# A fused vision tower on one core: two moves in TensorE's order of the last stage

## The reference

```python
h = window_attention(x)                     # 8x8 windows, 8 heads, rotary positions
h = h + local_attention(layernorm(h))       # 1024 tokens, 7x7 neighbourhood mask
h = h + routed_ffn(layernorm(h))            # expert by block of tokens, 2 expert layers
h = h + retention(layernorm(h))             # (q k^T * 0.99^(i-j)) v, no softmax
h = h + binary_experts(layernorm(h))        # below

gate = sigmoid(x @ proj_w.T + proj_b) > 0.5          # 8 gates for each token
w = einsum('be,eio->bio', gate, weight)              # a 64x64 matrix for each token
y = einsum('bi,bio->bo', sign(x), sign(w)) * scale
```

## Time and profile before

| | |
|---|---|
| time of the runs | 1646.99 us median of 3 (1640.81 to 1647.67) |
| profiled execution | 1643.16 us, span 1641.4 us |
| TensorE busy | 1514.8 us (92%) |
| ScalarE busy | 1005.4 us (61%), 8 or 9 tenths in the final stage |
| VectorE busy | 1207.1 us (74%) |
| final stage, first unit to the end | 903.7 to 1641.4 us |

### The profile page before, as it was taken

How to read it: one execution, slowest core, us unless ns; L and a number is a source line. 1 busy time by engine, 2 the same in 40 slices (tenths; PEclk the granted TensorE clock), 3 DMA queues, 4 the chain that set the end, 5 groups by cost and what they waited for, 6 DMA issues and landing times.

```text
span 1641.4 us, 85558 instructions
## 1 busy us (share of the span) xinstructions
PE 1514.8 (92%) x30828; PEld 1091.4 (66%) x30828; DVE 1207.1 (74%) x3605; ACT 1005.4 (61%) x1925; POOL 616.0 (38%) x926
## 2 busy tenths in 40 slices
PE   6899999799999999999878999999999999999997
PEld 5677777577877887778767565656656565656652
DVE  2566666578888888888648787888788787888862
ACT  2444444345555554555412888888888888888886
POOL 4252233366666676666522222222222222222210
PEclk9899999899999999999989999999999999999995
DMA  4322222244444444444411545455555555455553
GB/s 142 68 51 48 48 47 42 59 125 128 130 127 127 126 125 127 130 126 129 119 31 36 91 78 91 82 86 86 82 90 78 93 79 91 81 87 85 83 88 52
DMA packets 146869, 147.46 MB, mean 90 GB/s; under 512 B 54898, under 2 KB 102258, under 8 KB 146546
## 3 DMA queue, kind: packets, MB, share of 16 engines
q1 hardware_dynamic: 137922, 117.38, 37.5%
q10 hardware_dynamic: 8880, 29.16, 6.1%
HBM read 66.48 MB, written 16.99 MB: 51 GB/s over the span
## 4 chain that ended last, share of the span: by engine, by line
PE 77%; ACT 9%; issue 6%; SPq 3%; DMA 2%; DVE 1%; POOL 1%; ACTq 0%; POOLq 0%; DVEq 0%
PE ps_D L954 10%; PE ps_D L859 8%; PE ps_OT L878 4%; ACT prob L1267 4%; PE ps_AV L973 4%; PE ps_AV L886 3%; PE ps_D L708 3%; PE ps_D L855 3%; ACT prob L1162 3%; PE ps_J L1033 2%; PE ps_J L1017 2%; PE ps_OT L1043 2%; PE ps_OT L788 2%; PE ps_J L1067 2%; PE ps_OT L1110 2%
## 5 line engine op out<-in xcount | busy, mean ns | idle before, releaser
L1267 ACT ACTIVATE prob<-ps_D 128x1024 bf16<-128x1024 f32 x448 | 459.1, 1028 | 114.8 <-PE ps_D L954 114.2
L1237 ACT ACTIVATE prob<-ps_D 100x512 f32<-100x512 f32 x256 | 139.0, 595 | 101.5 <-PE ps_D L859 101.5
L577 POOL TENSOR_TENSOR tile_a<-q_st,q_mask 128x512 f32<-128x512 f32 x128 | 135.3, 1057 | 144.6 <-PE ps_D L859 138.6
L859 PE MATMUL ps_D<-tile_a,key_patch 64*100 64x128 f32 x2048 | 172.3, 287 | 0.1
L1443 DVE TENSOR_REDUCE m_sb<-ps_D 128x4 f32<-128x400 f32 x256 | 134.4, 565 | 22.2 <-PE ps_D L836 22.2
L1390 DVE TENSOR_REDUCE top<-ps_D 128x8 f32<-128x512 f32 x128 | 79.4, 683 | 96.5 <-PE ps_D L686 96.5
L551 POOL TENSOR_TENSOR rstd_bin<-veps_bin,minus_half 128x2 f32<-128x2 f32 x64 | 44.2, 690 | 260.5 <-DVE veps_bin L1328 260.5
L551 POOL TENSOR_TENSOR rstd_ret<-veps_ret,minus_half 128x2 f32<-128x2 f32 x64 | 47.4, 740 | 243.7 <-DVE veps_ret L1328 243.7
L859 PEld LDWEIGHTS ps_D<-tile_a,key_patch 64*100 64x100 f32 x2048 | 132.2, 165 | 0.0
L855 PE MATMUL ps_D<-mT,key_rows 64*100 64x128 bf16 x1024 | 118.6, 227 | 4.5 <-ACT prob L1237 4.5
L954 PE MATMUL ps_D<-tile_b,w_parts 64*64 64x256 bf16 x2048 | 104.6, 288 | 15.7 <-ACT prob L1267 12.2
(11 more groups left out here) (188 smaller groups left out, 3855.6 us busy)
## 6 DMA issues: line engine op xcount, KB each, us to landing
tile_a<-xg SPq DMA_DIRECT2D x192, 128.0 KB, 4.3
tile_b<-xg SPq DMA_DIRECT2D x192, 128.0 KB, 4.5
key_st<-k_d SPq DMA_DIRECT2D x128, 162.0 KB, 3.1
tile_b<-v_d ACTq DMA_DIRECT2D x128, 120.0 KB
tile_b<-v_d ACTq DMA_DIRECT2D x64, 160.0 KB
w_exp<-experts SPq DMA_DIRECT2D x64, 129.0 KB, 2.3
xT<-in_x SPq DMA_DIRECT2D x32, 256.0 KB
tile_a<-rot SPq DMA_DIRECT2D x256, 16.0 KB
```

Source lines behind the costliest of these rows:

```text
L577: gp.tensor_tensor(q_block[:, par, :].rearrange("c (p h q) -> c p h q", h=NH, q=NQ)[:, own, :, :], q_st[:, par, :].rearrange("c (p a q) -> ...
L859: mm = pe.matmul(s_loc[x][0:NKL, u * P:(u + 1) * P], key_patch[rows_of(x), par, at * NKL:(at + 1) * NKL], q_block[rows_of(x), par, at * P: ...
L1237: act.activation(prob1[0:NKL, 2 * g + x, :], s_loc[x][0:NKL, :], ACT.Exp).then_inc(T2["exp_done"], 1)
L1267: act.activation(sgn[:, k % 4, :], unit(k, par)[:, :], ACT.Sign).then_inc(BN["sign"], 1)
```

## The change

On TensorE, two groups of instructions are written at another place of the step. Unit 4 with its wait now stands ahead of the first expert product and its waits; it stood behind it. The next strip's unit 0, with its waits for the landed transfer and for the sign of unit 6, now stands directly behind unit 7, ahead of the retention output; it stood behind it. Nothing is added or removed, and the queues of the other engines are the same. `weights(4, ...)` is the fifth unit, `weights(0, ...)` the first one.

```diff
@@ -1026,15 +1026,15 @@
+                if q is not None:
+                    signed(q, 2)
+                    weights(4, par, unit(4, par))
                 if f is not None:
                     pe.wait_ge(FF["w_in"], times((f + 1) * 16))
                     pe.wait_ge(FF["hid_sb"], times(f * 3 + 1))
                     settle(pe)
                     pe.matmul(bank["J1"][:, 0:256], w_exp[:, 0, 0:HID], hidT[:, 0, :], start=True, stop=True).then_inc(FF["hid_ps"], 1)
 
-                if q is not None:
-                    signed(q, 2)
-                    weights(4, par, unit(4, par))
@@ -1101,6 +1101,15 @@
                 if q is not None:
                     weights(7, par, unit(7, par))
+                if n is not None:
+                    if isinstance(n, int) and n == 0:
+                        pe.wait_ge(s_placed, 13)
+                        pe.wait_ge(s_clear, 4)
+                    pe.wait_ge(BN["x_in%d" % (1 - par)], times((n + 1 + par) * 48))
+                if q is not None:
+                    signed(q, 6)
+                if n is not None:
+                    weights(0, 1 - par, ring(8, par))
                 filling(j, 3)
                 if r is not None:
                     pe.wait_ge(RT["sd"], times(r + 1))
@@ -1110,15 +1119,6 @@
                     mm.then_inc(RT["out_ps"], 1)
-                if n is not None:
-                    ...
-                    weights(0, 1 - par, ring(8, par))
```

More of the change, by code:

```diff
@@ L1112, in strips @@
                     mm.then_inc(RT["out_ps"], 1)
-                if n is not None:
-                    if isinstance(n, int) and n == 0:
-                        pe.wait_ge(s_placed, 13)
-                        pe.wait_ge(s_clear, 4)
-                    pe.wait_ge(BN["x_in%d" % (1 - par)], times((n + 1 + par) * 48))
-                if q is not None:
-                    signed(q, 6)
-                if n is not None:
-                    weights(0, 1 - par, ring(8, par))
             staggered(pe, strips)
```

## The result

Before and after ran on one chip, four executions each: before 1647.33 us (1640.81 to 1656.44), after **1623.9 us** (1619.42 to 1630.01), both medians. The ratio is 0.9863, with a 95% interval of 0.9825 to 0.9901, so the change saves 16 to 29 us. Medians are of all executions of a kernel; the ratios leave out one slow execution of experiment 1 (1636.92 us, at a granted clock of 0.967). The prediction was 1637, with a range of 1630 to 1648. The direction held; the time lies outside the range, at its fast side, and the gain of the medians, 23.4 us, is two and a half times the 9.4 us of the sum.

A forecast was written before the change was run, and what follows sets the result against it. The prediction took a step's time as TensorE's own work (92% busy) plus its waits; -0.41 + 0.25 = -0.16 us a step, times 59, is -9.4 us, giving 1637.6, stated as 1637, 8-in-10 range 1630 to 1648.

The forecast's parts named there:

- the 9.4 us of the sum: Whole change: 0.41 won and 0.25 lost make -0.16 us a step, times 59 steps.
- part 2: Unit 4 ahead of the first expert product fills TensorE's wait for `hidT`; query-key product 0.41 us a step earlier.
- part 1: Unit 0 ahead of the retention output: unit 1 and the clip come later, 0.25 us a step lost (bounds 0.19, 0.31).
- The base of 0.19: At unit 0: TensorE stands 0.19 us for sign 6, formerly covered by the retention output, so unit 1 comes later.
- The addition of 0.06: At unit 0: started out of a wait, it may last 0.53 us for 0.41, adding 0.12 in every second step.
- The signs that were announced: Changed kernel's timeline: expected waits and distances around `hidT`, the query-key product, unit 0, sign 0 and clip; clip starts 11.38 us apart.
- Nothing gained: Rival: unit 1's delay of 0.31 and a gain of only 0.32 a step cancel; 1646 us, chance 0.25.
- Both idle times pay: Rival: 0.34 at unit 2 and 0.25 at the product both won each step; 1612 us, within a 0.10 chance.
- A new wait that costs more than the fill: Rival: unit 0 waits for sign 6, bringing unit 1 over 0.41 us late; 1655 us, chance of slower 0.10.
- the bound of 0.22 a step: Fast bound of the whole change's summed gain: -0.22 us a step, -13 us.
- the case beyond it: Whole kernel: more gained than summed, up to both idle times, chance 0.10.

The follow-up runs named there:

- experiment 1: Kernel before with only unit 4 moved ahead of the first expert product, unit 0 left behind the retention output: 1625.82 us, ratio 0.9883.
- experiment 9: Kernel before with only unit 4 moved, and four transfers of gated tokens a step for six (part of the result left out): 1615.4 us, ratio 0.9821.
- experiment 6: Changed kernel with two extra 64x64x256 matmuls between the first expert product and the query-key product: 1643.84 us, one execution.
- experiment 2: Kernel before with only unit 0 moved ahead of the retention output, unit 4 left behind the first expert product: 1653.82 us, ratio 1.0056.
- experiment 5: Changed kernel with two extra 64x64x256 matmuls inside unit 5: 1624.82 us, one execution.
- experiment 4: Kernel before with unit 4 early, the retention output's second half behind the next unit 1, and `reduce(q, 2)` behind unit 7: 1611.9 us, ratio 0.9811.
- experiment 10: Kernel of experiment 4 with gated-token transfers issued ahead of the result's store on SyncE, and `yo` made behind the state update: 1607.41 us, ratio 0.9764.

## Why the prediction was wrong, point by point

**The step that failed: part 2's term of 0.41.** I followed the chain to the start of the query-key product and stopped there, taking all behind it to move as a block. Up to that point it was right: unit 4 came 0.37 behind the transposes (forecast 0.37), the product 0.34 behind it (0.34), the query-key product 0.53 behind that (0.51); 0.39 won for 0.41. Behind that point another 0.10 was won, since the query-key product no longer follows a 64x64 unit. Measured alone the part is worth 0.50 (experiment 9), and experiment 6 gives the missing piece back when a unit's kind of product is put in again (0.11 behind the query-key product). The rows to see it were there: two products of the same shape, 0.67 and 0.70 long, each behind a wait or a unit. I used their overlap for the first and did not ask what the second would be with a new neighbour. Net of the 0.02 short of 0.41, this is 0.08 of the missing 0.14 a step.

**The term that was too large: part 1's 0.25.** The base of 0.19 was right within 0.01 (1.83 - 1.64). The addition of 0.06 was for a first unit that lasts 0.53 when it is started out of a wait. It did not come: unit 0 lasts 0.41, and so does unit 3, which now starts out of a wait of 0.48. This is the other 0.06. It was no price before the change either: unit 3 starts 0.47 behind unit 2 both in the step where unit 2 lasts 0.53 (1205.64 to 1206.11) and in the one where it lasts 0.41 (1217.24 to 1217.71), since the clip holds it. What makes a unit 0.53 long in some steps was not tried and stays open; it is not the wait alone.

**In sum**: forecast -0.41 + 0.25 = -0.16; shown -0.39 - 0.10 + 0.19 = -0.30. Times 59 this is -17.7 us, which with 0.14 a step more than forecast puts the time at 1637.6 - 8.3 = 1629. The measured median of 1623.9 is 5 below that, and the interval of the ratio (1618 to 1631 on the median of before) holds it. I don't explain the 5 us: it is within the scatter of the executions; between the two that were profiled, 4.3 us lay ahead of the first sign.

**The signs that were announced.** The wait for `hidT` is gone. The query-key product starts 0.80 behind the modelled end of the transposes (1205.94 + 0.44 to 1207.18; forecast 0.75 to 0.85). Unit 0 stands 0.19 for a sign, though as a distance and not as a printed wait. Sign 0 follows sign 7 without a gap, unit 3 still starts 0.14 behind the clip, and TensorE now waits for the clip. All came, and the length of the step alone was off, 11.24 for 11.38. Each sign stood at a place that I had costed already; none stood behind the last of them.

**The rivals.** Nothing gained: its terms were a loss of 0.31 and a gain of 0.32, and both lay off. Both idle times pay: its time, 1612, lies 12 us from the measured 1623.9 and my 1637 lies 13 from it, but its mechanism is refuted, since the idle time at unit 2 was worth nothing (experiment 2). A new wait that costs more than the fill: it needed unit 0 to wait 0.41, and it waits 0.19. The loss from that wait is real (experiment 2, slower by 0.56%), and part 2 more than makes up for it. One effect stood in none of my cases: in the length of a step the changed kernel is only 0.06 longer than unit 4's move alone (11.24 against 11.18), and the two times can't be told apart (0.9863 and 0.9883, intervals overlap), since unit 4's gain alone runs into the landing of the transfers in every second step. Beside part 2, part 1 thus costs 0.06 and not its own 0.2.

**The range.** Its fast end came from the bound of 0.22 a step, and the case beyond it had 0.10. The bounds covered the terms that I had, and nothing covered a term that was missing. That a change moves a product of another shape out of a row of its like could be seen in the order of TensorE, and was worth a bound.

## What to carry to other kernels

When an instruction group is moved on TensorE, cost it to the second product behind the place that it leaves and the place that it enters, not to the first: a row of products of one shape and tile form is cheaper than the same products broken up, by 0.33 us for the one excursion of experiment 6. If a group of another kind has to stand somewhere, put it where a wait breaks the row already; that is what unit 4's move did. Before counting an idle time as gain, look for the wait that ends next on the same queue; here 0.33 at unit 2 was worth nothing, since the clip ended right behind, and of the clip's third of a microsecond the kernel before gave 0.06. And when a step gets shorter, ask which transfer had slack only because the step was long.

## What the runs showed of the hardware that I had not expected

- Two 64x64x256 bf16 products between two 128x128x256 fp32 products cost 0.43 us, and 0.10 within a unit of their own kind: 0.33 for leaving and coming back (experiments 5 and 6). About a third of it falls on the product behind, whose row lasts 0.70 for 0.59.
- The effect does not appear as a wait, but as busy time. A step of the same matmuls had 509.76 / 540 x 11.54 = 10.89 us of TensorE's busy time, and has 514.39 / 540 x 11.24 = 10.71. Of the 0.30 that a step is shorter, 0.18 were booked as work and 0.12 as idle.
- An engine's end and the first matmul that waited for it are 0.14 to 0.15 us apart in both kernels (sign 6 to unit 0, clip to unit 3).
- Six issues of one transfer each occupy SyncE's queue for 3.79 us. The kernel before, at 11.54 us a step, has no wait for their landing in its list; the changed kernel waits 0.23 in every second step, experiments 1 and 4 wait 0.41 and 0.48 in the rows shown. Where they are issued ahead of one store and `yo` is made later, one wait is left in 560 us (experiment 10).
